# Loading one activation table set, with logarithm and exponential together, ahead of ScalarE's first instruction

## The reference

```python
q = q / (jnp.linalg.norm(q, axis=-1, keepdims=True) + EPS)
k = k / (jnp.linalg.norm(k, axis=-1, keepdims=True) + EPS)
scores = jnp.einsum('bhnd,bhmd->bhnm', q, k) * scale
scores = jnp.where(allowed[None, None], scores, -jnp.inf)
attn = jax.nn.softmax(scores, axis=-1)
out = jnp.einsum('bhnm,bhmd->bhnd', attn, v)
return out.transpose(0, 2, 1, 3).reshape(B, N, D) @ out_w.T + out_b
```

## Time and profile before

| | us |
|---|---|
| median of 3 runs | 1313.18 |
| lowest and highest | 1312.51, 1313.33 |
| the profiled execution's own time | 1313.32 |
| its span in the trace | 1311.5 |
| TensorE, VectorE, ScalarE, GpSimd busy in it | 1121.8, 776.7, 667.6, 209.6 |

### The profile page before, as it was taken

How to read it: one execution, slowest core, us unless ns; L and a number is a source line. 1 busy time by engine, 2 the same in 40 slices (tenths; PEclk the granted TensorE clock), 3 DMA queues, 4 the chain that set the end, 5 groups by cost and what they waited for, 6 DMA issues and landing times. The chain is left out here.

```text
span 1311.5 us, 15297 instructions
## 1 busy us (share of the span) xinstructions
PE 1121.8 (86%) x5700; PEld 456.8 (35%) x5700; DVE 776.7 (59%) x1250; ACT 667.6 (51%) x1086; POOL 209.6 (16%) x125
## 2 busy tenths in 40 slices
PE   5577779899489888888888898999979857899998
PEld 3122243445212333333233233444434323244443
DVE  2444433734699999989899311202559889894200
ACT  3899952322603777777777555222475135431221
POOL 1101127010500000000000000000126432352000
PEclk8778879888855999999999989999989878899999
DMA  7000000001341011011000000000000000000000
GB/s 231 0 1 0 1 0 0 1 0 62 130 152 55 21 71 44 31 54 36 23 8 4 5 7 1 1 0 1 0 0 1 0 0 1 0 1 0 16 0 16
DMA packets 20767, 32.02 MB, mean 24 GB/s; under 512 B 6748, under 2 KB 14940, under 8 KB 20312
## 3 DMA queue, kind: packets, MB, share of 16 engines
q1 hardware_dynamic: 20696, 31.07, 6.9%
HBM read 23.23 MB, written 7.57 MB: 23 GB/s over the span
## 5 line engine op out<-in xcount | busy, mean ns | idle before, releaser
L1076 ACT ACTIVATE arena<-PS 128x384 f32<-128x384 f32 (+1 forms) x512 | 254.8, 549 | 169.2 <-PE PS L1051 168.7
L974 DVE CUSTOM_DVE_ANT_0 SQ<-PS,XP 128x1024 bf16<-128x1024 f32 x256 | 303.6, 1218 | 37.2 <-PE PS L964 37.2
L964 PE MATMUL PS<-arena 48*128 48x512 bf16 (+3 forms) x704 | 202.1, 358 | 20.2 <-DMA arena<-scr 12.8
L1051 PE MATMUL PS<-arena 50*128 50x512 bf16 (+3 forms) x640 | 164.0, 323 | 23.2 <-ACT arena L1076 15.7
L1067 PE MATMUL PS<-arena 128*32 128x512 f32 (+1 forms) x1280 | 138.3, 521 | 18.2 <-ACT arena L1082 17.2
L1502 ACT ACTIVATE arena<-PS,w_scl 128x512 f32<-128x512 f32 x64 | 43.7, 687 | 171.8 <-PE PS L1474 171.7
L1474 PE MATMUL PS<-arena,w_h1T 128*128 128x512 f32 x256 | 117.5, 605 | 13.9 <-ACT arena L1502 7.3
L1474 PE MATMUL PS<-arena,w_h2T 128*128 128x512 f32 x256 | 115.1, 595 | 0.0
L1051 PEld LDWEIGHTS PS<-arena 50*128 50x128 bf16 x640 | 44.8, 94 | 170.8 <-ACT arena L1076 156.2
L1696 DVE TENSOR_TENSOR_SCAN arena<-arena 128x512 f32<-128x512 f32 x64 | 83.5, 1305 | 0.1
L1519 DVE SCALAR_TENSOR_TENSOR XR<-PS,w_scl,XR 128x512 f32<-128x512 f32 x8 | 6.0, 749 | 130.3 <-PE PS L1483 130.3
(11 more groups left out here) (231 smaller groups left out, 1756.5 us busy)
## 6 DMA issues: line engine op xcount, KB each, us to landing
scr<-arena SPq DMA_DIRECT2D x16, 384.0 KB, 3.1
arena<-scr SPq DMA_DIRECT2D x64, 96.0 KB
arena<-scr SPq DMA_DIRECT2D x64, 64.0 KB
arena<-scr SPq DMA_DIRECT2D x64, 32.0 KB
XP<-xT SPq DMA_DIRECT2D x1, 1024.0 KB, 4.8
w_h1T<-h1T SPq DMA_DIRECT2D x1, 1024.0 KB, 6.8
w_h2T<-h2T SPq DMA_DIRECT2D x1, 1024.0 KB, 8.1
out_xT<-XR SPq DMA_DIRECT2D x4, 256.0 KB, 2.2
```

What stands on the lines that cost most here:

```text
L964: mm = t.matmul(PS[:, bank, k0 - lo:k1 - lo], packed(m, g, v, slice(q * P, (q + 1) * P), KP), packed(m, g, 2 + v, slice(k0, k1), KP), star ...
L974: v.tensor_tensor_reduce(JUNK[:, u % 2, :], PS[:, bank:bank + 2, :].rearrange("p a b -> p (a b)"), STRIP[:, at:at + S], 1.0, -3.0e38, ALU. ...
L1051: mm = t.matmul(PS[:, S_BANKS[e % 2], at:at + b_ - a_], packed(n, g, 2 + v, slice(kt * P, (kt + 1) * P), KP + MROWS), packed(n, g, v, slic ...
L1076: nc.scalar.activation(PT[:, T % 2, HEADS[i], a0_:a1_], PS[:, S_BANKS[e % 2], a0_:a1_], ACT.Exp).then_inc(s_free, 1)
```

## The change

One line is added at the start of ScalarE's program. It loads, by its name, the set that holds logarithm and exponential together.

```diff
         @block.scalar
         def _(a):
+            nc.scalar.preload_act_table_set("natural_log_exp_and_others")
             wait_loads(a, 0)
             ln_act(a, 0)
             wait_loads(a, 1)
```

## The result

Four runs of the changed kernel took 1256.53 us in the median (1246.97 to 1258.02), the kernel before beside them 1313.26 (1312.51 to 1314.34). The ratio is 0.9552, 95% interval 0.9503 to 0.9601, so the change takes off 56.7 us, where 61.4 were forecast. The profiled execution took 1258.02 us, with a span of 1256.2: 55.3 less than before.

The account below looks back on a forecast made before the run. ScalarE, with its table loads, was taken to bound the first attention, and TensorE after the change. Gains of 3.9, 12.3, 31.8, 11.9 and 1.5 us sum to 61.4, so 1313.3 becomes 1252, range 1244 to 1264.

Parts of the forecast that it names:

- ScalarE bounds the attention, and the loads are almost half of it: First attention: ScalarE busy 36.43 of a middle chunk's 37.31 us, 17.96 of it 14 table loads; 18.5 without them.
- The first norm, 3.9: Ahead of window 0's scores: three bare loads at 1.29 us each go, gain 3.9 us, scores at 33.6.
- the rival of a switch at twice its row: A switch costs 2.57 us, shown only in the first norm: 3.9 us more gain, 1248; chance 0.03.
- The middle chunks, TensorE at 20.9 and 0.5 of handovers: Chunks 1 and 2: TensorE becomes the bound, 21.4 us each instead of 37.31, gain 31.8 us.
- Some 2 us of cover: GpSimd's scaling, 4.42 us a chunk, would end some 2 us before the next chunk's scores need it.
- Chunk 0, 22.4: First chunk: TensorE's need 16.1, 2.5 us for half clock, 3.8 for norm gaps; 22.4 against 34.75, gain 12.3 us.
- Chunk 3, 19.8: Last chunk: 16.8 us of TensorE's work plus unfilled gaps and tail, 19.8 against 31.73, gain 11.9 us.
- The last projection, 3.82: Output projection after the last chunk: 3.82 us at full clock instead of 5.32, gain 1.5 us.
- Behind the attention, plus or minus 2 and counted as nothing: Unchanged programs after the attention, 1127.5 us: clock changes may move it by 2 us either way, counted as nothing.
- The clock did not stay at 0.81: Rival: TensorE's granted clock in the attention stays as before, 13 us less gain, 1265; chance 0.08.
- The functions did not get slower: Rival: ScalarE's functions cost more from the common set, at a factor of 2.2 the time is 1322; chance 0.01.
- Every load counts: Rival: 55 bare loads at 1.29 us each give 71 us, 1241 in all; chance 0.04.

Follow-up runs that it names:

- version without the collision: Changed kernel with the scaling of the queries moved from GpSimd to VectorE and v's copy put ahead of the masks: 1244.35 us.
- the changed kernel's third trace: The changed kernel run again with nothing edited, beside the kernel before: 1255.17 us.
- with TensorE kept busy: Changed kernel with 7 matmuls whose result nobody reads added on TensorE ahead of the first scores: 1246.11 us.
- the dose curve: Changed kernel with loads of the same set put back, 5 or 10 in a chunk: 1266.7 us and 1288.43 us.

## Why the prediction was right, and where it was not

The forecast was 1252 in a range of 1244 to 1264; 1256.5 was measured, 4.7 us of gain less. The path is right: the loads were the bound, and without them TensorE comes close to being it. That the total came out so near is in part luck, since the stretch behind the attention alone differs by 12 us between executions; the 59.2 us against 61.4 up to the next layer norm are the better test. Three of the signs that the prediction named for being wrong did occur: a clock of 0.95 in chunk 1, a TensorE that waits for VectorE (2.25 us in chunk 0, 0.33 in chunk 2), and 3.9 us more behind the attention. Step by step:

**ScalarE bounds the attention, and the loads are almost half of it: right.** ScalarE's 17.4 and 17.9 us in chunks 1 and 2 are 1.1 and 0.6 under the forecast 18.5, with one or two activations less between the cuts, and the activations have kept their length.

**The first norm, 3.9: right.** The wait fell by 3.84, and where TensorE's clock fell as early as before, window 0 starts at 33.57 (forecast 33.6). That also settles the rival of a switch at twice its row: three removed loads gave three rows, nothing booked elsewhere. The page "ScalarE: Activation LUTs" of the Trainium skill (section "What ACT_TABLE_LOAD costs"), with its drain of some 1380 ns beside each load, would have given 8.0; the trace does not agree with it. **The load at the start, nothing: right.** The first square now starts at 8.60 us, and TensorE's sums start at 12.17 behind its centring matmuls.

**The middle chunks, TensorE at 20.9 and 0.5 of handovers: the number was near (21.92, and 22.62 with half clock at its start), the reason for the last 0.8 us was not.** Leaving out 1.91 us of TensorE's work left chunk 2 at 21.92. TensorE's own need was well worked out (21.1 in the kernel without the scaling). What the step lacks is the collision of GpSimd's scaling with VectorE's masks, 21.92 - 21.15 = 0.77 us a middle chunk. "Some 2 us of cover" was asked of the scaling's own end, and of that it was true: window 0's scores of the next chunk did not wait for it. The question that was not asked is what the longer overlap does to the masks.

**Chunk 0, 22.4: 1.5 too low, by the same term.** Without the scaling it is 22.2; with it the stretched masks lengthen a wait on TensorE from 1.20 to 2.25 us, and half clock follows that reaches into chunk 1. That 22.4 fits the kernel without the scaling is two errors that cancel. The start at half clock was put at 2.5 us, and taking it away gave 1.5 in the version without the collision (22.05 to 20.56) and 1.6 over chunks 0 and 1 with it. The 20.56 us at full clock leave 4.5 above TensorE's forecast need of 16.1, where 3.8 were put down for the gaps of the norm. **Chunk 3, 19.8: right** (20.13). **The last projection, 3.82: 0.3 too high** (3.51).

**Behind the attention, plus or minus 2 and counted as nothing: mis-sized.** Over the fourteen profiled executions of this study it took from 1119.4 to 1131.4 us, with the same instructions there; the one after was the highest, 3.9 over the one before. This term should have had a range some 12 us wide, as is the spread of the changed kernel's thirteen runs (1246.37 to 1258.02). The mechanism is TensorE's clock: this stretch is longer where more of it ran at half clock, 140 us of it at the low end and 160 at the high one. The 3.9 us are no price of the change: in the changed kernel's third trace the stretch takes 1127.7 us, as before the change. What remains open is what sets where the clock falls, why the kernel before keeps within 4 us over all its runs (1311.1 to 1315.1; 1127.6 and 1127.7 us behind the attention in its two traces) while the changed one takes either end, and whether the kernels that fell near 1120 do so by their making. Most kernels here have one trace each. For the same reason, of the 8 to 11 us by which the last versions are shorter than the changed kernel, only what they gain in the attention is shown to be theirs: 1.6 us with TensorE kept busy, 3.2 without the collision, 4.7 with both.

**The other rivals.** The clock did not stay at 0.81: it was 0.86, 0.95, 1.00 and 1.00 in the four chunks. The functions did not get slower. "Every load counts" fails by the dose curve.

The Trainium skill has the collision, in "SBUF — State Buffer", section "SBUF: two separate sides": a VectorE instruction with two inputs from SBUF and a GpSimd instruction that reads SBUF take one shared pair of ports, and whichever starts first keeps it for its whole length. The trace agrees. In chunk 2 of the kernel after, the four scalings last 1.42, 1.88, 1.88 and 1.03 us (1.04 alone) and the three masks beside them 1.29, 1.92 and 1.39 (1.09 alone, 0.68 for the short one). Their ends alternate, a scaling at 95.56 us, a mask at 96.50, a scaling at 97.40, a mask at 98.35, a scaling at 99.25: no two of them finish closer than 0.9 us, as when each waits for the other's instruction. None grew by more than 0.85 us, less than one instruction of the other engine. The VectorE instructions with an input from PSUM did not grow. The prediction did not draw on that page.

## What to carry to other kernels

When a bound is removed, the next one need not be the engine with the next most work: list which pairs of engines will newly run at the same time, and look in the trace of before for a place where they already touch (here one pair of masks of 2.58 us among pairs of 2.09). Put a load that serves several functions first wherever a chain alternates between them, and price it from a place where it lies bare and not from the sum of all loads. In a kernel that TensorE bounds for long stretches, the part that a change does not touch can differ between executions by more than the forecast's error (here 12 us), so judge the change by the stage that it touches as well as by the total.

## What was not expected of the hardware

- VectorE's masks with both inputs in SBUF: 2.09 to 3.14 us a pair, 1.28 to 1.99 a short pair, beside GpSimd's elementwise instructions, which went from 4.42 to 6.11 for four. Both lose.
- The same scaling, 128 x 512 in f32, takes 0.42 us as VectorE's tensor_scalar and 1.1 us as GpSimd's tensor_tensor alone.
- Loading the table set that is already loaded takes the whole 1283 ns.
- TensorE's granted clock differs in time from run to run of one kernel, and a stretch of some 222 matmul records took 76.7, 80.1 or 82.0 us by it.
